# A two-layer graph attention kernel: row maxima of chunk 6 in four pieces, t ahead of s, E in two halves

## What is computed

```python
# layer 0 (E: 4096 x 64 entity embeddings)
s, t = (x @ W0) @ a0[:64], (E @ W0) @ a0[64:]
e = leaky_relu(s[:, None] + t[None, :], 0.2)
h = softmax(where(adj > 0, e, -9e15), axis=1) @ E
x = layernorm(x + elu(h + x))
# layer 1
wh = x @ W1
s, t = wh @ a1[:64], wh @ a1[64:]
e = leaky_relu(s[:, None] + t[None, :], 0.01)
x = layernorm(x + softmax(where(adj > 0, e, -1e9), axis=1) @ wh + bias)
```

## Time and profile before

| | us |
|---|---|
| runs, median of 3 | 635.17 (633.31 to 636.13) |
| the profiled execution | 634.35 |
| its span | 632.5 |
| DVE busy | 558.5 (88%) |
| ACT busy | 540.3 (85%) |
| PE busy | 503.1 (80%) |
| POOL busy | 161.4 (26%) |
| mean granted TensorE clock | 0.973 |

### The profile page before, as it was taken

How to read it: one execution, slowest core, us unless ns; L and a number is a source line. 1 busy time by engine, 2 the same in 40 slices (tenths; PEclk the granted TensorE clock), 3 DMA queues, 4 the chain that set the end, 5 groups by cost and what they waited for, 6 DMA issues and landing times.

```text
span 632.5 us, 14283 instructions
## 1 busy us (share of the span) xinstructions
PE 503.1 (80%) x6039; PEld 234.2 (37%) x6039; DVE 558.5 (88%) x764; ACT 540.3 (85%) x626; POOL 161.4 (26%) x105
## 2 busy tenths in 40 slices
PE   1307667989989799999988977588888888899994
PEld 0204344434443334433445533243333333333352
DVE  4899999999799998989768897969988998889795
ACT  0869995999999997899989989578997999779883
POOL 1080100366026650277001001006101430121050
PEclk9999998989999999999999989689999999999997
DMA  8998985866667746550100100000000000000000
GB/s 196 406 362 297 348 317 194 278 237 220 227 207 268 260 141 235 191 168 2 35 20 1 37 2 2 28 8 2 10 8 28 1 18 16 4 1 18 1 19 10
DMA packets 18252, 76.16 MB, mean 120 GB/s; under 512 B 6300, under 2 KB 8524, under 8 KB 9996
## 3 DMA queue, kind: packets, MB, share of 16 engines
q1 hardware_dynamic: 17384, 74.89, 33.9%
q0 software_dynamic: 112, 0.28, 0.2%
q10 hardware_dynamic: 692, 0.08, 0.1%
HBM read 74.16 MB, written 1.09 MB: 119 GB/s over the span
## 4 chain that ended last, share of the span: by engine, by line
issue 29%; DVE 28%; PE 21%; ACT 18%; POOL 2%; DMA 1%; SPq 0%; POOLq 0%; ACTq 0%; DVEq 0%
ACT Pm L802 15%; DVE junk L932 14%; PE acc L1210 12%; PE zps L1271 6%; DVE zps L1089 5%; DVE v L909 3%; PE acc L1217 2%; ACT zps L794 2%; DMA VE<-in_L_gnn_entity_embs 1%; PE zps L1180 1%; POOL tAB L556 0%; DVE tot L996 0%; DVE tot L1001 0%; DVE Pm L841 0%; DVE s_col L1036 0%
## 5 line engine op out<-in xcount | busy, mean ns | idle before, releaser
L802 ACT ACTIVATE Pm<-zps,ebias 128x1024 f32<-128x1024 f32 (+1 forms) x320 | 291.8, 933 | 49.8 <-DVE zps L1089 44.4
L794 ACT ACTIVATE zps<-S_row,ntau_col 128x1024 f32<-128x1024 f32 (+1 forms) x210 | 200.0, 955 | 5.7
L1271 PE MATMUL zps<-D,v 128*128 128x128 bf16 x2048 | 164.3, 224 | 32.7 <-ACT zps L794 18.3
L1271 PEld LDWEIGHTS zps<-D,v 128*128 128x128 fp8e4 x2048 | 119.1, 99 | 173.2 <-ACT zps L794 82.1
L1210 PE MATMUL acc<-Pm,X 128*32 128x512 f32 (+2 forms) x1280 | 142.1, 532 | 31.0 <-ACT Pm L802 27.4
L1210 PE MATMUL acc<-Pm,VE 128*32 128x512 f32 (+2 forms) x1280 | 144.9, 525 | 24.2 <-ACT Pm L802 17.2
L932 DVE CUSTOM_DVE_ANT_0 junk<-v,adj_in 128x2048 int8<-128x2048 int8 (+3 forms) x80 | 153.9, 1951 | 3.6 <-ACT adj_in L681 3.6
L932 DVE CUSTOM_DVE_ANT_0 junk<-v,u_row 128x2048 int8<-128x2048 int8 x64 | 155.3, 2439 | 0.2
L1089 DVE SCALAR_TENSOR_TENSOR zps<-S_row,tau_col,zps 128x1024 f32<-128x1024 f32 (+1 forms) x110 | 113.4, 1052 | 40.3 <-PE zps L1271 39.6
L1217 PE MATMUL acc<-Pm,ones 128*32 128x256 f32 (+1 forms) x1280 | 86.1, 341 | 0.0
L539 POOL TENSOR_TENSOR tAB<-flag,totW 128x520 f32<-128x520 f32 (+1 forms) x7 | 9.9, 1409 | 234.4 <-issue 138.0
(11 more groups left out here) (170 smaller groups left out, 247.1 us busy)
## 6 DMA issues: line engine op xcount, KB each, us to landing
adj_in<-in_adj SPq DMA_DIRECT2D x62, 1024.0 KB, 6.2
S_row<-S_rows_scratch SPq DMA_DIRECT2D x6, 512.0 KB, 4.1
Pm<-in_adj SPq DMA_DIRECT2D x2, 1024.0 KB, 7.5
S_row<-S_rows_scratch SPq DMA_DIRECT2D x3, 256.0 KB, 3.1
out<-tAB SPq DMA_DIRECT2D x3, 256.0 KB, 2.6
adj_in<-u_row_scratch SPq DMA_DIRECT2D x2, 256.0 KB, 3.5
S_row<-S_rows_scratch POOLq DMA_DIRECT2D x1, 256.0 KB, 8.6
out<-tAB SPq DMA_DIRECT2D x2, 128.0 KB, 2.0
```

The source lines that it names most:

```text
L794: a.activation(mask_of(n), S_row[:, C % 2, 0:R(C) * P], ACT.Relu, bias=ntau_col[:, layer(C), n % JT:n % JT + 1]).then_inc(seed_done, 1)
L802: a.activation(Pm_of(k, 0, R(C) * P), mask_of(k), ACT.Exp, bias=ebias[:, layer(C), int(seeded(k)), J:J + 1])\
L1271: last = t.matmul(mask[:, r * P:(r + 1) * P], v[:, chunks[C][1] + r, J * P:(J + 1) * P], D[:, C % 2, PART * second + r, :], start=(r * P % ...
```

## The change

- The row maxima of chunk 6 are in four pieces (1536, 1024, 1024, 512 columns). The first piece of 10 instead of 8 row tiles of chunks 5 and 6 stands in chunk 3; chunk 4 has the last two of these and five of the new second pieces; chunk 5 the other three and the eight third pieces (THIRD), in steps 0, 1, 5, 9 and 12.
- In chunk 4 scores and rows stand at steps 13 and 21 (were 15 and 22), the late pieces of chunk 5 at 22 to 25 (were 24 to 27). The second diagonals stand at step 21 of chunk 5 (was 20).
- Chunk 5 has 28 seeds (was 27), with step 1 now seeded; in chunk 4 the unseeded steps 25, 26, 27 become 24, 25, 26; chunk 6 keeps 20 seeds, of which two are now steps 1 and 3.
- In `scores`, t is made before s, and u's diagonals before s; PE spreads u before it turns s; ACT saves u, then s, three steps ahead of the rows step instead of one behind it.
- E comes in two transfers, and product and sum are made per half; ACT saves half of u before each of its first two conversions.

The diff, with a line of context:

```diff
@@ -21,7 +21,7 @@
 WIDTHS = ((4, 8, 8, 8, 4), (4, 8, 8, 8, 4))
-SEEDS = ((29, 28, 28, 26, 24), (27, 20, 20, 10, 0))
+SEEDS = ((29, 28, 28, 26, 24), (28, 20, 20, 10, 0))
@@ -48,7 +48,9 @@
     LAG, NARROW_LAG = 2, 4
-    SETUP_AT = 2
+    E_HALVES = slice(0, JT // 2), slice(JT // 2, JT)
@@ -59,21 +61,22 @@
     AFTER_WIDE = dict(reciprocal=7, elu=10, sums=13, squares=17, scores=22, rows=25)
-    IN_LAST = dict(add_up=6, elu=8, normalise=10, scores=15, rows=22)
-    IN_FIRST = dict(add_up=4, elu=6, normalise=9, scores=12, rows=17, maxima=18, second=20, weights=22)
-    THIRD = (0, 1, 5, 9, 12, 20, 21, 21)
+    IN_LAST = dict(add_up=6, elu=8, normalise=10, scores=13, rows=21)
+    IN_FIRST = dict(add_up=4, elu=6, normalise=9, scores=12, rows=17, maxima=18, second=21, weights=22)
+    THIRD = (0, 0, 1, 1, 5, 9, 9, 12, 12, 12, 12)
     IN_LAYER_1 = dict(reciprocal=7, sums=13, squares=18)
+    ROWS_LEAD = 3
     BEHIND_FIRST = 2
-    BEFORE_LAST = (19, 20, 21, 22, 23, 26, 27, 28)
-    EARLY = (3, 4, 5, 7, 11, 12, 13, 17)
-    LATE_AT = 24
+    BEFORE_LAST = (19, 20, 21, 22, 23, 24, 26, 27, 28, 29)
+    EARLY = (3, 4, 5, 7, 11, 12, 15, 16, 17, 18, 19)
+    LATE_AT = 22
@@ -199,7 +202,7 @@
         w_loaded = [sem("w_loaded0"), sem("w_loaded1")]
-        e_loaded, x_loaded = sem("e_loaded"), sem("x_loaded")
+        e_loaded, x_loaded = [sem("e_loaded0"), sem("e_loaded1")], sem("x_loaded")
@@ -262,7 +265,7 @@
             elif C == NC + 1:
-                ends = [0, third, KNOWN * P, N]
+                ends = [0, third, first_spread, KNOWN * P, N]
@@ -275,7 +278,7 @@
                     if J == at("rows", C):
-                        users += [("rows", C - 1)] + [("u", C - 1)] * (C - 1 in SPREAD)
+                        users += [("u", C - 1)] * (C - 1 in SPREAD) + [("rows", C - 1)]
@@ -341,8 +344,8 @@
-            first = JT * C if C == LAST or not narrow(C) else 0
-            may = [k for k in range(JT * C + 2 * (first < JT * C), JT * (C + 1)) if (users_before["step", k] or C == 0)
+            first = JT * C if C == LAST or not narrow(C) and C != NC + 1 else 0
+            may = [k for k in range(JT * C + 2 * (first < JT * C and C < NC), JT * (C + 1)) if (users_before["step", k] or C == 0)
@@ -402,8 +405,12 @@
             return 20 if C == NC - 2 else 27
-        known_first = [(NC, r, 0) for r in range(R(NC))] + [(NC + 1, r, 0) for r in range(R(NC + 1))]
-        assert len(EARLY) == len(known_first) - len(BEFORE_LAST) + R(NC)
+        by_first = [(NC, r, 0) for r in range(R(NC))] + [(NC + 1, r, 0) for r in range(R(NC + 1))]
+        by_second = [(NC, r, 1) for r in range(R(NC))] + by_first[len(BEFORE_LAST):] + \
+            [(NC + 1, r, 1) for r in range(R(NC + 1))]
+        by_third = by_second[len(EARLY):] + [(NC + 1, r, 2) for r in range(R(NC + 1))]
+        assert len(by_third) == len(THIRD)
@@ -411,16 +418,15 @@
                 return [(nxt, i // 2, i % 2) for i in range(n) if i * halves_within(C) // n + 1 == J] + \
-                       [piece for piece, step in zip(known_first, BEFORE_LAST) if step == J]
+                       [piece for piece, step in zip(by_first, BEFORE_LAST) if step == J]
             if C == NC - 1:
-                early = [(NC, r, 1) for r in range(R(NC))] + known_first[len(BEFORE_LAST):]
-                return [piece for piece, step in zip(early, EARLY) if step == J] + \
+                return [piece for piece, step in zip(by_second, EARLY) if step == J] + \
...
                 n = R(nxt)
-                return [(nxt, r, 1) for r in range(n) if THIRD[r] == J] + \
+                return [piece for piece, step in zip(by_third, THIRD) if step == J] + \
                        [(NC, r, 3) for r in range(R(NC)) if at("maxima", C) + r // 2 == J] + \
-                       [(nxt, r, 2) for r in range(n) if at("weights", C) + r * 6 // n == J]
+                       [(nxt, r, 3) for r in range(n) if at("weights", C) + r * 6 // n == J]
@@ -486,7 +492,9 @@
             sp.dma_start(wraw[:, 0, :], W0).then_inc(w_loaded[0], 16)
-            sp.dma_start(VE[:, :, :], E.rearrange("(n p) f -> p n f", p=P)).then_inc(e_loaded, 16)
+            for half, tiles in enumerate(E_HALVES):
+                sp.dma_start(VE[:, tiles, :], E.rearrange("(n p) f -> p n f", p=P)[:, tiles, :])\
+                    .then_inc(e_loaded[half], 16)
@@ -756,11 +764,11 @@
             a.activation(warm[:, :], tanh_bias[:, :], ACT.Tanh, bias=tanh_bias[:, :], scale=40.0)
-            for H in range(SETUP_AT):
+            for H in range(2):
+                for g in range(H * JT // GT // 2, (H + 1) * JT // GT // 2):
+                    save_u(g, slice(g * GT * P, (g + 1) * GT * P))
                 convert(H)
-            for g in range(JT // GT):
-                save_u(g, slice(g * GT * P, (g + 1) * GT * P))
-            for H in range(SETUP_AT, AHEAD):
+            for H in range(2, AHEAD):
@@ -774,10 +782,10 @@
                             elu_exp(C - 1)
-                        if layer(C - 1) == 0 and J == at("rows", C) + 1:
-                            save_rows(C - 1)
+                        if layer(C - 1) == 0 and J == at("rows", C) + (1 if C - 1 not in SPREAD else -ROWS_LEAD):
...
                                 save_spread_u(C - 1)
+                            save_rows(C - 1)
@@ -837,9 +845,11 @@
             dve.wait_ge(wbc_saved, 1)
-            dve.wait_ge(e_loaded, 16)
-            link(d.tensor_tensor(prod, VE[:, :, :], wbc[:, 1, :].unsqueeze(1).broadcast_to([P, JT, F]), ALU.mult))
-            link(d.tensor_reduce(t_col[:, :], prod, AX.X, ALU.add))
+            for half, tiles in enumerate(E_HALVES):
+                dve.wait_ge(e_loaded[half], 16)
+                link(d.tensor_tensor(prod[:, tiles, :], VE[:, tiles, :],
+                                     wbc[:, 1, :].unsqueeze(1).broadcast_to([P, JT // 2, F]), ALU.mult))
+                link(d.tensor_reduce(t_col[:, tiles], prod[:, tiles, :], AX.X, ALU.add))
@@ -987,7 +997,7 @@
                 dve.wait_ge(turned, JT * (C + 1))
-                dve.wait_ge(uS_ready, C + 2)
+                dve.wait_ge(uT_ready, C + 2)
@@ -1005,19 +1015,21 @@
                 xc = xcols(C)
+                xs, h, tAf, tBf = tiles_of(C)
...
                         scale(dve, d, C)
-                    xs, h, tAf, tBf = tiles_of(C)
                     dve.wait_ge(new_done, C + 1)
-                    d.tensor_tensor(tAf, xs, per_feature(wbc[:, 2, :], C), ALU.mult).then_inc(sprod_done, 1)
                     d.tensor_tensor(tBf, xs, per_feature(wbc[:, 3, :], C), ALU.mult).then_inc(tprod_done, 1)
-                dve.wait_ge(sprod_done, C + 1)
-                link(d.tensor_reduce(s_col[:, xc], tA[:, 0:R(C), 0:F], AX.X, ALU.add))
...
                 dve.wait_ge(uS_turned, C + 1)
-                d.tensor_scalar(uS[:, 0, 0:R(C)], t_col[:, xc], uoff[:, 1:2], None, ALU.add)
+                d.tensor_scalar(uS[:, 0, 0:R(C)], t_col[:, xc], uoff[:, 1:2], None, ALU.add).then_inc(uT_ready, 1)
+                if C in SPREAD:
+                    u_diagonals(C)
+                    d.tensor_tensor(tAf, xs, per_feature(wbc[:, 2, :], C), ALU.mult).then_inc(sprod_done, 1)
+                dve.wait_ge(sprod_done, C + 1)
+                link(d.tensor_reduce(s_col[:, xc], tA[:, 0:R(C), 0:F], AX.X, ALU.add))
@@ -1076,7 +1088,6 @@
                                 cols = slice(0 if C == NC - 1 else KNOWN, xcols(C - 1).stop)
-                                u_diagonals(C - 1)
@@ -1256,9 +1267,9 @@
                         if J == at("rows", C):
-                            turn_rows(C - 1)
...
                                 spread_u(C - 1)
+                            turn_rows(C - 1)
```

## The result

| | us |
|---|---|
| after, median of 9 runs | 630.48 (627.08 to 632.74) |
| before, same chip, 9 runs | 633.94 (633.31 to 636.13) |
| ratio after / before | 0.9932, 95% interval 0.9912 to 0.9952 |
| profiled execution after (before: 634.35) | 630.16, span 628.3, granted clock 0.973 |
| busy DVE, ACT, PE, after | 559.5, 541.7, 504.9 (each within 2 of before) |

The account below looks back on a forecast made before the run. Bound by stage: DVE from 24 to 65 us, ACT in chunks 4 and 6, no engine full in chunk 5. -1.9 + 3.0 - 6.6 - 1.6 = -7.1 from 634.35 gives 627.2, median 628.0; range 624.3 to 632.5.

Parts of the forecast that it names:

- Chunk 5, -6.6: Chunk 5, from its own start: the 6.7 us stall goes, -0.55 by seeding step 1, +0.65 new ACT waits; bounds -8, -4.
- a matter of order in DVE's queue: Chunk 5, steps 21 and 22: ACT's 6.7 us stall blamed on two 2048-column maxima queued ahead of the second addition.
- rival (c): Chunk 5: the stall moves instead of going, chunk worth only -1, total -1.5, 633.7 us; chance 0.10.
- the 0.65 for ACT's waits at step 14: Chunk 5: ACT, saving u and s earlier, waits about 0.4 us for u and 0.25 for s.
- Chunk 4, +3.0: Chunk 4: DVE's fuller queue delays the additions of steps 24 to 26, so ACT ends 3.0 us later; bounds 0, +5.
- Chunk 3, 0: Chunk 3: two added pieces (3.4 us) fall where DVE idles and behind its addition, costing nothing; bounds 0, +1.
- Start, -1.9: Start: E in halves saves 2.3 us, less about 0.4 for one more issue; bounds -2.3, +1.4.
- DVE is full from there to about 119, so what it starts sooner it ends sooner: Start: the claim that the 1.9 us gained there lasts, as DVE has no idle time until about 119 us.
- rival (b): Start: the transfers bind it (share 0.92), so +1.4 in place of -1.9, 631.3 us; chance 0.11.
- Chunk 6, -1.6: Chunk 6: ACT makes seeds at steps 1 and 3 where it waited, DVE's last diagonals 1.6 us sooner; bounds 0, -3.
- (a): Chunk 4 hides its work: the three late additions cost nothing, total -10.1, 625.0 us; chance 0.12.
- (d): Chunk 5: ACT's waits in chunk 4 starve PE, whose clock stays at 1.2 GHz: up to +14.8, 642.7 us; chance 0.03.

Follow-up runs that it names:

- Experiment 10: Changed kernel with two 1024-column maxima of chunk 5 moved from step 12 to step 21, between the additions of steps 21 and 22: 630.95 us, ratio 0.9932.
- Experiment 9: Changed kernel with ACT's saves of u and s in chunks 4 and 5 one step behind the rows step, as before: 629.69 us, ratio 0.9914.
- experiment 8: Changed kernel with the last two middle maxima of chunk 4 moved from steps 18 and 19 to step 31: 628.40 us, ratio 0.9904.
- experiment 3: Changed kernel with E in halves, but ACT making both conversions ahead of all of u, as before: 631.23 us, ratio 0.9937.
- `start_only`: Kernel before with only E's halves and ACT's new order of saves and conversions at the start: 633.22 us, ratio 0.9978.
- `no_start`: Changed kernel with E's halves and ACT's new order at the start undone: 631.49 us, ratio 0.9956.
- experiment 6: Changed kernel with 22 instead of 20 of chunk 6's steps seeded by ACT: 628.62 us, ratio 0.9895.
- `gap31_c6_22`: Changed kernel with two middle maxima of chunk 4 moved to step 31 and 22 seeds in chunk 6: 627.69 us, ratio 0.9889.

## Why the prediction was right, and where it was off

The direction, the range and the main mechanism held; the median came out 2.5 us above the forecast. The change itself was worth only half of what was forecast, 3.5 us for 7.1: the forecast was laid from a median of 635.17 (3 runs), and the 9 runs of the same kernel had 633.94. Chunks 4 and 5 came out as forecast within 1 us; what is missing lies in the start and in chunk 6. By its steps:

- **Chunk 5, -6.6: right (-7.4).** No wait at steps 21 and 22, clock 1.00. One sentence of its first part was wrong: the stall was called "a matter of order in DVE's queue". Experiment 10 puts two maxima back between the additions and no stall comes. The stall went because addition 22 comes 8.3 us sooner in the chunk. The 5.0 us less in the queue, which rival (c) was answered with, are not all of it: with them alone it would end at 32.3 (36.6 - 5.0 + 0.66, an estimate), and by the prediction's own time for exponential 22 (396.6, 30.8 into the chunk) ACT would still have waited 1.5. DVE's waits for the copy of u (2.28) and for the power (0.89) had to go too. Experiment 9 shows that the earlier save isn't needed for it (DVE then waits 0.72 for u and no stall comes), and no run tells apart what the shorter queue, the pieces moved ahead of u, and t ahead of s each give. Most of the 0.8 us more than forecast is the 0.65 for ACT's waits at step 14, which did not come: the scores start at 383.02, 1.8 us sooner than 382.14 shifted by 2.7 (forecast 0.6), 1.1 of it from the shorter power on POOL. The Trainium skill, page "SBUF — State Buffer", section "SBUF: two separate sides", has GpSimd, when an instruction of VectorE with two SBUF inputs has started first, shut out until that instruction ends. The trace agrees: the power's 1.96 us are its 1.01 alone and about 1 us of a maximum of 1.23.
- **Chunk 4, +3.0: right**, and in the changed kernel by its mechanism: the last addition stands as late in DVE's queue as worked out. Taking 2.3 us out of that queue (experiment 8) gives back only 0.9, since ACT and PE come right behind. There the 1.1 us of ACT's waits for u and s, which the prediction rightly put at nothing behind a longer wait, count in full.
- **Chunk 3, 0: right.**
- **Start, -1.9: its size failed, in both directions.** The gain at u was 3.1: E's second half was ready when DVE came for it at 9.06, where the whole had landed at 9.96. But "DVE is full from there to about 119, so what it starts sooner it ends sooner" did not hold. DVE had never waited for one of these transfers because it came just late enough, by less than 0.1 us (experiment 3); up to 3.1 us sooner, it waits 1.3 and 3.1. That is rival (b) in part, but not by what its +1.4 was made of: loads issued later. The two loads behind the first conversions were issued 0.8 and 2.1 later, but the load in question 1.25 sooner; it only didn't gain as much as DVE. Behind it, when the clock is low in chunk 1 at the wrong place, another 1.4 are lost. Profiled starts of the same program end at -0.3 and +0.8; `start_only` and `no_start` put its worth at 0.8 and 1.0 us (medians: 634.00 less 633.22; 631.49 less 630.48, the latter over two batches).
- **Chunk 6, -1.6: wrong, +0.6.** The step that failed is "I put its last diagonals 1.6 sooner, ACT's end 2.5 sooner, and take the smaller". Two seeds at steps 1 and 3 fill ACT's waits, but the number of additions stays 12, as before, and two of them move from where DVE idles to where it is full. With the number raised to 22 as well (experiment 6) the 1.4 come.
- **Rivals.** (a) failed: chunk 4 does not hide its work. (b) in part. (c) failed. (d): ACT's waits in chunk 4 did not bring chunk 5 to the low clock; it ran at 1.00 where it had 0.86. The low stretch inside the stall (0.50) is there in both kernels that have the stall, before and `start_only`. The clock didn't make the gain: `gap31_c6_22` has 0.76 in 366 to 380 and 0.57 in 388 to 396, without a stall, and its chunk 5 still takes 7.0 less.

What stays open: why the same transfer takes 6.6 us in one execution and 8.3 in another (the share is 0.95 and 0.93); and why the clock's low stretch leaves chunk 8 with 22 or 24 seeds in chunk 6 (three profiles of three) and in none of the others.

## What to carry to other kernels

When an engine "never waits" for a stream, ask by how much: here it was less than 0.1 us, and a stage with a transfer share of 0.92 gave back only about a third of the 3.1 us that its start had gained. A seed or any work moved onto a waiting engine helps only if the other engine's work falls away where it is full; count its idle time in that part of the stage, not over all of it. And what makes a late instruction late in an in-order queue is all that stands ahead of it, the work and the engine's own waits: add up both, and when a queue is shortened, look for what becomes full next (experiment 8).

## What the hardware showed that I had not expected

- The granted clock's low stretches (level 1.2 GHz) fall at different places in executions of one program, and the place decides the price: at 103 to 113 us the kernel before has 0.83 and loses nothing, but a stretch that reaches past 113 costs 1.4 to 1.5 us in 7 of 7 profiles. The runs of the changed kernel spread over 5.7 us (627.1 to 632.7), those of the kernel before over 2.8. The start alone doesn't explain it (`start_only` spreads over 2.9, `no_start` over 2.4), and what does isn't shown. One profile is not enough for a difference of 1 or 2 us between such kernels.
- A transfer of 1 MB into the same buffer, waited for at the same place, made DVE stand 1.3 us in one execution of the changed kernel and 3.1 us in another. From issue to landing it took 6.6 and 8.3 us.
